# The bias of the first layer norm made by DVE in one instruction, and all z items of the loop made by POOL

## The reference, cut to what matters

```python
def _ln_c(v, eps=1e-6): return (v - mean(v, -1)) / sqrt(var(v, -1) + eps)
def _ln_t(v, eps=1e-5): return (v - mean(v, -1)) / sqrt(var(v, -1) + eps)
x = x + conv_ref(_ln_c(x), wq, bq, wk, bk, wv, bv, wo, bo, gamma, beta)
#   conv_ref: channel attention per image (Gram matrix over h*w, softmax inside 8 heads),
#   then a row norm of the result with gamma and beta
t = to_tokens(x)
t = t + ffn_ref(_ln_t(t), gate_w, gate_b, w1, w2)
#   ffn_ref: a softmax over all tokens for each of 64 experts, the best 8 tokens of each,
#   two small layers on them, and a scatter-add back
```

## Time and profile before

| | |
|---|---|
| median of 3 runs | 2142.67 us (2136.2 to 2142.91) |
| profiled execution, its own time | 2155.56 us |
| its span | 2153.8 us |
| busy in the span | POOL 1939.2, ACT 1882.0, PE 1873.0, DVE 1822.8 us |
| core clock of PE granted, mean | 0.957 |

### The profile page before, as it was taken

One profiled execution on the slowest core, in us unless ns is written; L12 is line 12 of the kernel. 1 busy time (PEld: TensorE's weight loads), 2 busy tenths in 40 slices (PEclk: granted clock), 3 DMA queues, 4 the chain that ended last, 5 costly groups with the idle time before them and its releaser, 6 DMA issues.

```text
span 2153.8 us, 42420 instructions
## 1 busy us (share of the span) xinstructions
PE 1873.0 (87%) x11917; PEld 1286.6 (60%) x11917; DVE 1822.8 (85%) x4612; ACT 1882.0 (87%) x5020; POOL 1939.2 (90%) x2068
## 2 busy tenths in 40 slices
PE   6999999999999999999999999999999987636991
PEld 6866666666666666666666666666666643213570
DVE  4689999999999898989899999999999899624670
ACT  6899999999999999999999999999999987743420
POOL 5799999999999999999999999999999999961387
PEclk9999999999999999999999999999999998765995
DMA  5498888887888888888788888888788676694963
GB/s 188 157 262 222 228 223 206 226 229 216 218 218 235 224 227 210 224 231 222 215 216 231 229 224 220 212 229 227 213 222 223 178 182 162 165 263 124 282 104 32
DMA packets 111068, 447.92 MB, mean 208 GB/s; under 512 B 10575, under 2 KB 52404, under 8 KB 61684
## 3 DMA queue, kind: packets, MB, share of 16 engines
q1 hardware_dynamic: 81140, 302.61, 42.9%
q0 software_dynamic: 29696, 142.61, 34.2%
HBM read 306.78 MB, written 138.41 MB: 207 GB/s over the span
## 4 chain that ended last, share of the span: by engine, by line
ACT 38%; POOL 21%; issue 17%; PE 16%; DVE 5%; ACTq 1%; DMA 1%; POOLq 0%; SPq 0%; DVEq 0%
ACT U L553 16%; POOL U L430 8%; POOL U L435 7%; ACT zT L516 6%; ACT UT L510 6%; PE G L747 4%; ACT LTS L580 3%; ACT LTS L525 3%; PE T L729 3%; PE O L680 2%; POOL zn L451 2%; POOL out_dram L490 2%; PE T L736 1%; ACT zn L574 1%; POOL U L442 1%
## 5 line engine op out<-in xcount | busy, mean ns | idle before, releaser
L553 ACT ACTIVATE U<-xa,nA,rA 128x128 f32<-128x128 f32 x1948 | 803.7, 483 | 2.1 <-issue 1.3
L747 PEld LDWEIGHTS G<-UT 128*128 128x128 f32 x4096 | 536.8, 192 | 226.5 <-issue 225.3
L430 POOL TENSOR_TENSOR U<-U,bet 128x512 f32<-128x512 f32 x512 | 651.4, 1272 | 2.2
L435 POOL TENSOR_TENSOR U<-U,rO 128x512 f32<-128x512 f32 x512 | 532.2, 1040 | 20.3 <-ACT rO L533 19.3
L747 PE MATMUL G<-UT 128*128 128x128 f32 x4096 | 542.0, 275 | 0.0
L680 PE MATMUL O<-U,MT 128*128 128x512 f32 x1024 | 529.5, 599 | 3.0 <-DVE U L938 3.0
L451 POOL TENSOR_TENSOR zn<-U,rZ 128x512 f32<-128x512 f32 x414 | 446.6, 1079 | 11.0 <-ACT rZ L564 10.3
L936 DVE BATCH_NORM_STATS2 stO<-O 128x6 f32<-128x256 f32 x1024 | 386.8, 423 | 50.2 <-PE O L680 49.5
L729 PE MATMUL T<-ident,U 128*128 128x128 f32 x2048 | 324.3, 281 | 119.1 <-ACT UT L510 108.6
L729 PEld LDWEIGHTS T<-ident,U 128*128 128x128 f32 x2048 | 224.6, 142 | 318.1 <-issue 314.1
L954 DVE BATCH_NORM_STATS2 stA<-xa 128x6 f32<-128x256 f32 x1024 | 386.8, 426 | 31.8 <-DMA xa<-in_x 28.5
(11 more groups left out here) (151 smaller groups left out, 1655.0 us busy)
## 6 DMA issues: line engine op xcount, KB each, us to landing
xa<-in_x SPq DMA_DIRECT2D x128, 1024.0 KB, 6.3
U<-in_x POOLq DMA_DIRECT2D x128, 1024.0 KB, 10.8
out_dram<-U SPq DMA_DIRECT2D x128, 1024.0 KB, 8.6
U<-in_L_ffn_weight SPq DMA_DIRECT2D x112, 256.0 KB
LTS<-in_L_ffn_weight SPq DMA_DIRECT2D x16, 256.0 KB
xa<-out_dram,UT POOLq DMA_INDIRECT x64
out_dram<-U,UT POOLq DMA_INDIRECT x64
zT<-in_L_ffn_weight SPq DMA_DIRECT2D x1, 128.0 KB
```

The costliest lines, as they stand in the source:

```text
L430: gp.tensor_tensor(rows(a, i), rows(a, i), bet_b, ALU.add).then_inc(S["gb"], 1)
L435: gp.tensor_tensor(rows(a, i), rows(a, i), rO[:, i // 2 % 2, i % 2 * TI:(i % 2 + 1) * TI].unsqueeze(2).to_broadcast([P, TI, W]), ALU.mult) ...
L553: last = sc.activation(utile(a, i, j), xa[:, k % XR, h * W:(h + 1) * W], ACT.Identity, scale=rA[:, k % 2, h:h + 1], bias=nA[:, k % 2, h:h ...
L747: last = te.matmul(G[:, 0:P], v, v, start=(i == 0 and j == 0), stop=(i == NI - 1 and j == TI - 1))
```

## The change

The two instructions of POOL at `L_NMU` are replaced by one of DVE (mean times -1 times root), with the same waits, at the head of DVE's step. `Z_ITEMS` becomes empty, so that the 43 items that ACT made into z among the first 452 (three an image for 14 images, and one) go to POOL.

```diff
-Z_ITEMS = (3, 11, 27)
+Z_ITEMS = ()
...
 # POOL's body
-                    if r := item(b, t, L_NMU, IC):
-                        a, k = r
-                        pool.wait_ge(S["a_rstd"], cnt(a, NK, k + 1))
-
-                        wait(pool, S["u_ready"], cnt(a, NI, IC * (k - 1)))
-                        wait(pool, S["u_pool"], min(cnt(a, NI, IC * (k - 1)), SHARED))
-                        gp.tensor_tensor(nA[:, k % 2, :], stA[:, k % 2, :, 1], rA[:, k % 2, :], ALU.mult).then_inc(S["a_nmu"], 1)
-                        pool.wait_ge(S["a_nmu"], cnt(a, 2 * NK, 2 * k + 1))
-                        gp.tensor_scalar(nA[:, k % 2, :], nA[:, k % 2, :], -1.0, None, ALU.mult).then_inc(S["a_nmu"], 1)
...
 # DVE's body, first thing in a step
+                    if r := item(b, t, L_NMU, IC):
+                        a, k = r
+                        dve.wait_ge(S["a_rstd"], cnt(a, NK, k + 1))
+
+                        wait(dve, S["u_ready"], cnt(a, NI, IC * (k - 1)))
+                        wait(dve, S["u_pool"], min(cnt(a, NI, IC * (k - 1)), SHARED))
+                        ve.scalar_tensor_tensor(nA[:, k % 2, :], stA[:, k % 2, :, 1], -1.0, rA[:, k % 2, :],
+                                                ALU.mult, ALU.mult).then_inc(S["a_nmu"], 1)
```

More of the change, by code:

```diff
@@ L420, in body @@
                         k = i // IC
-                        pool.wait_ge(S["a_nmu"], cnt(a, 2 * NK, 2 * k + 2))
+                        pool.wait_ge(S["a_nmu"], cnt(a, NK, k + 1))
                         for j in range(TI - shared(a, i), TI):
@@ L539, in body @@
                         act.wait_ge(S["a_ln"], cnt(a, NK, k + 1))
-                        wait(act, S["a_nmu"], cnt(a, 2 * NK, 2 * (k - 1)))
+                        wait(act, S["a_nmu"], cnt(a, NK, k - 1))
                         wait(act, S["u_pool"], min(cnt(a, NI, IC * (k - 1)), SHARED))
@@ L545, in body @@
                         k = i // IC
-                        act.wait_ge(S["a_nmu"], cnt(a, 2 * NK, 2 * k + 2))
+                        act.wait_ge(S["a_nmu"], cnt(a, NK, k + 1))
                         if a[0] >= 2:
@@ L948, in body @@
                             dve.wait_ge(s_x[k % XR], base if it is None else it * 64 + base)
-                            wait(dve, S["a_nmu"], cnt(a, 2 * NK, 2 * (k - 1)))
+                            wait(dve, S["a_nmu"], cnt(a, NK, k - 1))
                         for n in range(TI // 2):
```

## The result

The changed kernel has a median of 2356.93 us (2354.88 to 2358.4, 4 runs) against 2141.95 us of the kernel before (2136.2 to 2142.91, 4 runs). The ratio is 1.1015, with a 95% interval of 1.0998 to 1.1032. The profiled execution has a span of 2353.9 us.

What follows compares the result with a forecast made beforehand. ACT bounds the kernel before, DVE the changed one: 13.7 images x (113.2 + 0.3 - 113.8) gives -4.1 us, the early part -3.4, so 2142.67 - 7.5 = 2135 us, range 2110 to 2162.

Steps and rivals of the forecast that it cites:

- What bounds the kernel, and what each engine needs: Main loop: ACT sets the pace at 113.8 us an image; after the change ACT needs 110.3, POOL 108.6, DVE 113.2.
- The forecast's sign for a sum by engines being the wrong tool: Main loop: DVE still waiting 50 us in 1200 while ACT waits too would mean they lose time in turn.
- The wait inside the instruction: DVE's two-SBUF-input product stands inside itself, counted busy, until POOL's current instruction is over; no view of waits shows it.
- The failed step: DVE's new product: a blocked one costs the rest of one POOL instruction plus 0.07 us; 0.7 us taken, eight an image.
- 113.2 + 0.3: Main loop, us an image: DVE's need with eight products at 0.7, plus 0.3 for what stays of its waits.
- The second rival: DVE's products meet POOL in a bad phase, each costing 0.95 to 1.1 us: +25 us, 2168 us, chance 0.27.
- The wait for the maximum: ACT's exponential (L571) waits for DVE's negated maximum; ACT's busy share falls to 95 to 97%.
- The early part: Between first y and first z POOL sets the pace; four biases at 0.87 us leave it, 3.4 us saved.

Runs made afterwards that it cites:

- The run with the wait: Changed kernel, with POOL waiting once a chunk, behind the DMA issue, for its own last z to be written: 2117.19 us, ratio 0.9886.
- z alone: Kernel before, with only the list of ACT's z items emptied and POOL keeping its pair: 2167.99 us, ratio 1.0053.
- the reduction with eight waits: Changed kernel, DVE's bias made by a one-input reduction, POOL waiting for its last z once a chunk: 2116.28 us, ratio 0.9815; again 2105.36 us, 0.9839.
- The run with two waits: Changed kernel, DVE's bias made by a one-input reduction, POOL waiting for its last z only at steps 24 and 28: 2103.25 us, ratio 0.9838.
- the run with the reduction alone: Changed kernel, DVE's bias made by a reduction with one SBUF input, no wait added on POOL: 2183.75 us, ratio 1.0134.

## Why the prediction was wrong, by its steps

*What bounds the kernel, and what each engine needs.* Right. ACT's new need of 110.3 us an image, POOL's 108.6 and DVE's 107.6 without the product came within 1 us an image of most runs without many long instructions. The run with the wait has 112.3 us an image between like exponentials (466.82 and 1477.47, nine apart) where DVE at 0.67 us each needs 107.6 + 5.4 = 113.0; z alone has 114.3 (440.62 and 1469.63) where POOL needs 114.8; the reduction with eight waits has 111.4 (458.46 and 1460.92) where POOL, with 0.36 us a wait, needs 111.5. The run with two waits has 111.5 where ACT needs 110.3, the largest miss. DVE's base of 107.6 may be too high by some 0.6, since it holds one product of 0.75 (L1018) that takes 0.17 in the run with the wait. Even the changed kernel comes out close once the price is the measured one: from 400 to 1600 us the product has a mean of 2.51, 107.6 + 20.1 makes 127.7, and DVE's 41.7 us of waits add 4.5, so 132.2 an image where the trace has 130.0. The forecast's sign for a sum by engines being the wrong tool, DVE waiting 50 us in 1200 while ACT waits too, was nearly there (41.7), and the sum held all the same; the price put into it did not.

*The wait inside the instruction.* Right that DVE stands inside its instruction, counted as busy, while POOL computes: the product of 4.47 us ends at 1028.65, 0.04 us after POOL's beta. Not right that it stands there for one instruction of POOL; this one stood over four. The product of two tiles (up to 12.4 us), TENSOR_SCALAR with its one input (up to 7.0) and the cast (up to 7.3) were held, the reduction (at most 0.25) was not. What in an instruction decides this no run here shows.

*The failed step.* "The price of a blocked one is then what is left of POOL's instruction plus some 0.07 us". I read this from L1018, whose sixteen samples all lay in a program in which POOL's pair ended the overlap once a chunk, and carried it to a program from which the change takes that pair away. The term was sized at 0.7 us and measured 2.25: 52 of 116 were held past the ends of 4 to 11 POOL instructions, where the step allowed one. With the pair's effect put back by a wait it measures 0.67, and an image takes 112.3 us where the forecast had 113.2 + 0.3: the forecast describes that kernel rather than this one, and is 18 us too slow for it (2117 against 2135). The decisive thing was not in what the change adds but in what it removes: I had booked the pair's inner wait as 0.78 us of POOL's time to be saved, and its use as a break was not on the list.

The profile before held a hint: the cast's longest, 2.32 us, was held past the end of beta and of the next y (from 1861.87 to 1864.19), so more than one.

*The second rival* had the right side and the wrong size, +25 us at 1.0 us each; it too allowed no more than one POOL instruction to be waited for.

*Does the sum close?* From the run with the wait to the changed kernel, the products take 288.4 - 85.8 = 203 us more, and the two profiled executions differ by 2353.9 - 2124.2 = 230 us (240 by the medians). The rest, some 27 us, I have not split; waits that the engines pass on to one another and the lower clock of PE (0.94 on the mean from 400 to 1600 us against 0.99) may both stand in it.

*The wait for the maximum* is where I put it (L571, 30.4 us from 400 to 1600), but the waits for the statistics of O (L520, 52.9) and for PE's banks (L671, 51.6) are larger, and ACT's busy share fell to 84.7%, not to 95 to 97. *The early part* went the right way: from the first y to the first z POOL took 129.68 - 90.45 = 39.2 us before and 127.94 - 91.05 = 36.9 in the changed kernel, 2.3 of the 3.4 us forecast.

## What to carry to other kernels

Before an instruction of DVE is priced beside a busy POOL, ask whether POOL ever stands still, and whether the change takes away what makes it stand: a dependent pair, a semaphore wait, a gap. Behind each DMA issued by POOL, one wait for its own last result cost 0.36 us, and the eight an image were worth some 240 us here; and a negated product by a reduction over two neighbouring elements was not held up at all. A duration's minimum, median and maximum side by side (158, 808, 1078, or 171, 172, 2321) say more than its mean: here such a spread on a fixed shape was a wait that no view of waits lists.

## What the runs showed of the hardware that I had not expected

- In the records POOL's instructions overlap by 0.03 to 0.05 us after a wait, and by 0.12 to 0.28 us more behind each DMA that POOL issues, until it next has to wait; up to 1.16 us more were seen (a y of 2.19 us in the run with the reduction alone, 1.03 at rest). The distance from start to start stays the same (0.99 to 1.00 for y and z).
- In that state DVE's product was held over up to eleven POOL instructions (12.4 us), its TENSOR_SCALAR of 128x16 up to 7.0 us and its cast of 128x8 up to 7.3 us; its reduction of 128x32 into 128x16 never was (247 ns at most in four runs). A stop of POOL of 0.07 us was enough to let DVE in. The holding also occurred, far more seldom, with an overlap of 0.03 to 0.1 us (7 products of 3.7 to 11.1 us, with SP issuing the DMA).
- The version with the reduction and POOL's waits is 1.6 to 1.9% faster than the kernel before (0.9839 and 0.9815 in two timings), and computes the same.
